# A four-layer graph network on one core: attention rows scattered whole in f32, and the counting pass with one accumulator

## The chip, the cores and the metric

The kernel runs on one NeuronCore of one Trainium2 chip. The metric is the device time of one execution in microseconds (us). Five engines work side by side from queues of their own: TensorE (PE; its weight loads are listed as PEld), VectorE (DVE), ScalarE (ACT), GpSimd (POOL) and SyncE (SP), which here only starts transfers. They wait for each other by semaphores.

## The reference, cut to what matters

The graph has 6250 nodes with 64 features and 206,250 edges (src, dst). Four layers follow each other, each on relu(layernorm(x)), each added to x. The first two are the ones that the change touches:

```python
# layer 0: attention, 4 heads of 16 channels
h = (x @ W).reshape(n, HEADS, CH)
e = leaky_relu(a_src[src] + a_dst[dst], NEG_SLOPE)
e = exp(e - segment_max(e, dst)[dst])
s = segment_sum(e, dst)
out = segment_sum(h[src] * (e / s[dst])[:, :, None], dst)
# layer 1: sum over the neighbours, divided by the root of the degree
agg = segment_sum(vertices[src], dst)
deg = segment_sum(ones, dst)
agg = agg * (clip(deg, 1.0, None) ** (-0.5))[:, None]
return agg @ weight.T + bias
```

Layer 2 sums rows weighted by edge_weight, and layer 3 runs two relational convolutions.

## The kernel before, in words

The nodes lie in 49 windows of 128. A first stage sorts the edges on the chip, so that the edges into one window of destinations stand in 50 columns of 128 edges (column c holds edges whose source is in window c, and column 49 the overflow). A window's columns are worked in 6 groups of 10, 8, 8, 8, 8 and 8 columns. Then come the passes over all 49 windows: attention, count, weight, and two relation passes. Each is a hardware loop over windows, whose body holds the six groups written out; each engine's queue is in order, and the semaphores named below are all that ties one engine to another.

**Gather and scatter are products with one-hot matrices.** A gather product takes the one-hot matrix of a column's sources (OT) and the rows of a window, and gives a row for each edge; a scatter product takes the one-hot matrix of the destinations (OD) and the edges' rows, and sums them into the 128 nodes of the window. Since products of bf16 are not exact enough for f32 rows, a row is split into three bf16 parts (high, middle, low) whose sum is the f32 number: Hp holds a window's rows as three parts.

**Attention pass** (`edge_pass`). For a column, PE's `gather` issues three products of 72 columns (L1157: 64 features and 8 scores, three parts) and three of 8 columns (L1161: the destination's part of the score, from `tab`, into the last 8 columns). DVE takes the scores (`scores`, L2040), ACT the exponent (`exponents`, L826), and DVE multiplies the rows by it (`weigh`, L2052) into Wf, 68 f32 columns for each edge. To scatter, Wf is split: ACT copies the high part (`highest`, L817), DVE subtracts it (`rest`, L2075), ACT copies the middle part (`middle`, L822), POOL subtracts again for the low part (`lowest`, L637). PE's `scatter` (L1175) then issues one bf16 product of 204 columns for each column of edges, and three more (L1182) for the few edges left over by the sort. The three parts of the sum stand side by side in PSUM; `evict` adds them on DVE (L2084) and adds the result to agg (L2090), twice for each window, as groups 0 to 2 use one PSUM bank and groups 3 to 5 another. DVE also makes both one-hot matrices (L2023 for OT, from codes that a DMA brings; L1657, a helper's line that every pass uses, for OD) and three small ones for the left-over edges (`few`, L2095).

On PE the body goes: gather of group g+2, scatter of group g. On DVE: `weigh` g, the OT matrix of g+3, `rest` g, `scores` g+1, the OD matrix of g+1, and an `evict` behind groups 2 and 5. A gather waits for `weigh` two groups before it (two sets of PSUM banks), a scatter for f_low of POOL.

**Count pass** (`count_pass`). PE builds a 128x128 matrix of edge counts for each column from two one-hot matrices (`build`, L1289), ACT copies it to bf16 (L884), and PE applies it to Hp (`apply`, L1304, 193 columns: three parts of 64, and a column of ones that gives the degree); L1311 is for the left-over edges. Groups 0 to 2 sum in PSUM bank 6 and groups 3 to 5 in bank 7. DVE makes both one-hot matrices of a group (L1657 twice), and evicts each bank with three instructions (L2272, L2276, L2277), each of which waits for the one before (`flink`); the evictions stand behind groups 2 and 5.

**Weight pass** (`weight_pass`, not changed). Groups 0, 2 and 4 of a window are scattered whole: an f32 one-hot matrix times f32 rows of 64 columns (L1229, and L1236 for the left-over edges), and groups 1, 3 and 5 in three bf16 parts (L1247, 192 columns). Its gather is L1215, three products of 64 columns for each column. An f32 product shows in the trace as two weight loads and two matmuls.

## Time and profile before

| what | value |
|---|---|
| median of 3 runs | 6114.63 us (6114.55 to 6117.37) |
| the profiled execution, its own time | 6114.21 us |
| its span in the trace | 6112.5 us |
| busy in the span: PE, DVE, ACT, POOL | 4598.9, 4985.0, 3358.9, 1454.7 us |
| attention pass, about | 1530 to 2732 us |
| count pass, about | 2795 to 3336 us |
| weight pass, about | 3399 to 4076 us |

A busy share is of one engine in one stretch. Matmuls overlap in their records, since the end of one is later than the start of the next; so the price of one in a row of them is the distance from start to start, not its mean duration. PEclk is the clock that TensorE was granted, as a share of its full speed.

### The profile page before, as it was taken

The numbers are of one execution on the slowest core, as the hardware profiler recorded it, in microseconds if no ns is written. First come the engines' busy times: TensorE is split into PE (matmuls) and PEld (weight loads), VectorE is DVE, ScalarE is ACT, GpSimd is POOL, SyncE is SP. The second block draws the span as 40 slices with busy tenths as digits, with TensorE's granted clock in tenths as the row PEclk, the third lists the DMA queues.
The fourth block names the chain that finished last, engine by engine and source line by source line (L and its number), as shares of the span: only waits on it lengthen the run. The fifth ranks groups of instructions, "written<-read, shape, count | busy, mean of one in ns | idle before, by whom it ended". The sixth has DMA issues, their size and how long they took to land.

```text
span 6112.5 us, 245738 instructions
## 1 busy us (share of the span) xinstructions
PE 4598.9 (75%) x91050; PEld 3703.5 (61%) x91050; DVE 4985.0 (82%) x10975; ACT 3358.9 (55%) x9701; POOL 1454.7 (24%) x2032
## 2 busy tenths in 40 slices
PE   2566666663777777765776799978999997999997
PEld 1343444342667666754666799976666665666665
DVE  8999999998999999998888899986666665666665
ACT  3566666562333333335666333346777776777776
POOL 2555555552333333320000222210000000000000
PEclk7677777776777778778999899989999998999999
DMA  1000000000666666640000344423232322333322
GB/s 43 1 1 1 1 1 1 1 1 16 216 200 203 202 202 201 203 150 11 0 0 0 108 118 118 120 73 93 84 84 84 84 84 78 84 84 85 84 84 75
DMA packets 305216, 501.29 MB, mean 82 GB/s; under 512 B 76918, under 2 KB 78454, under 8 KB 305126
## 3 DMA queue, kind: packets, MB, share of 16 engines
q1 hardware_dynamic: 303782, 499.39, 28.0%
q8 instruction: 59, 0.97, 0.1%
q0 software_dynamic: 576, 0.52, 0.0%
q10 hardware_dynamic: 768, 0.16, 0.0%
q14 instruction: 31, 0.25, 0.0%
HBM read 408.40 MB, written 91.57 MB: 82 GB/s over the span
## 4 chain that ended last, share of the span: by engine, by line
issue 54%; DVE 30%; PE 6%; POOL 6%; DVEq 2%; DMA 1%; ACT 1%; POOLq 0%; ACTq 0%; SPq 0%
DVE agg L1693 7%; DVE arena L1657 6%; POOL arena L637 5%; DVE Hp L1657 3%; DVE arena L1699 2%; DVE tmp L1657 2%; PE PS L1215 2%; PE PS L1229 1%; PE PS L1247 1%; DVE arena L2163 1%; DVE arena L2171 1%; PE PS L1236 1%; DVE arena L2272 1%; DVE arena L2282 0%; DVEq L1663 0%
## 5 line engine op out<-in xcount | busy, mean ns | idle before, releaser
L1657 DVE TENSOR_TENSOR arena<-iotab,arena 128x1024 bf16<-128x1024 bf16 (+6 forms) x1813 | 1688.5, 958 | 559.3 <-PE PS L1371 471.6
L932 ACT ACTIVATE arena<-PS 128x384 bf16<-128x384 f32 x2450 | 1077.2, 492 | 509.2 <-PE PS L1364 496.4
L1371 PE MATMUL PS<-arena 32*128 32x193 bf16 (+1 forms) x41552 | 1080.6, 243 | 1.2 <-ACT arena L932 1.2
L768 ACT ACTIVATE arena<-PS,m 128x196 bf16<-128x196 f32 x1813 | 743.5, 429 | 548.8 <-POOLq L537 328.5
L1371 PEld LDWEIGHTS PS<-arena 32*128 32x128 bf16 x41552 | 815.6, 93 | 180.2 <-issue 140.4
L1364 PE MATMUL PS<-Hp,arena 128*128 128x192 bf16 (+1 forms) x4900 | 662.5, 250 | 114.0 <-DMA arena<-hots 58.9
L1045 PE MATMUL PS<-arena,tmp 128*128 128x262 bf16 x1813 | 507.2, 328 | 294.3 <-DVE tmp L1657 293.1
L1037 PE MATMUL PS<-agg,onesb 128*128 128x196 bf16 x1715 | 514.4, 301 | 200.4 <-ACT arena L768 195.9
L1157 PE MATMUL PS<-Hp,arena 128*128 128x72 bf16 x7350 | 548.3, 214 | 63.3 <-DVE arena L2023 40.7
L1038 PE MATMUL PS<-Hp,own_b 128*128 128x196 bf16 x1813 | 545.9, 305 | 55.1 <-DVE Hp L1657 53.8
L714 POOL TENSOR_TENSOR arena<-arena 128x512 bf16<-128x512 f32 x98 | 168.8, 1722 | 1743.4 <-ACT arena L942 1743.4
L637 POOL TENSOR_TENSOR arena<-arena 128x544 bf16<-128x544 f32 (+1 forms) x294 | 391.5, 1332 | 797.1 <-ACT arena L822 796.9
L1175 PE MATMUL PS<-arena 128*128 128x204 bf16 x2450 | 351.1, 302 | 285.1 <-POOL arena L637 283.9
L1364 PEld LDWEIGHTS PS<-Hp,arena 128*128 128x128 bf16 x4900 | 326.4, 98 | 343.8 <-ACT arena L932 151.4
L1161 PE MATMUL PS<-tab,arena 128*128 (+1 forms) x7350 | 530.2, 172 | 0.0
L913 ACT ACTIVATE arena<-PS,ewB 128x64 f32<-128x64 f32 x1176 | 257.4, 330 | 428.1 <-PE PS L1215 428.1
L1157 PEld LDWEIGHTS PS<-Hp,arena 128*128 128x128 bf16 x7350 | 436.5, 105 | 90.5 <-DVE arena L2023 40.8
L1693 DVE TENSOR_TENSOR agg<-Hp,agg 128x196 bf16<-128x196 bf16 x1666 | 458.6, 275 | 17.1
L817 ACT ACTIVATE arena<-arena 128x544 bf16<-128x544 f32 (+1 forms) x294 | 198.7, 676 | 484.8 <-DVE arena L2052 484.8
L1161 PEld LDWEIGHTS PS<-tab,arena 128*128 128x128 bf16 x7350 | 459.3, 109 | 4.8
L1175 PEld LDWEIGHTS PS<-arena 128*128 128x128 bf16 x2450 | 249.7, 116 | 320.2 <-issue 218.1
L1045 PEld LDWEIGHTS PS<-arena,tmp 128*128 128x128 bf16 x1813 | 200.2, 113 | 376.9 <-DVE tmp L1657 358.5
(362 smaller groups left out, 9065.4 us busy)
## 6 DMA issues: line engine op xcount, KB each, us to landing
arena<-hots SPq DMA_DIRECT2D x735, 256.0 KB, 2.6
arena<-codes SPq DMA_DIRECT2D x245, 512.0 KB
hots<-arena SPq DMA_DIRECT2D x245, 256.0 KB, 4.2
arena<-hots SPq DMA_DIRECT2D x147, 320.0 KB, 2.9
arena<-codes SPq DMA_DIRECT2D x49, 640.0 KB
hots<-arena SPq DMA_DIRECT2D x49, 320.0 KB, 4.5
rows_h<-Hn SPq DMA_DIRECT2D x4, 1568.0 KB, 9.2
rows_l<-Y SPq DMA_DIRECT2D x1, 1764.0 KB, 10.4
```

The lines of the kernel that those rows point to most:

```text
L637: pool.tensor_tensor(W3[g % 2][:, 0:sz, 2 * v:3 * v], Rf[g % 2][:, 0:sz, 0:v], W3[g % 2][:, 0:sz, v:2 * v], ALU.subtract).then_inc(f_low, 1)
L768: act.activation(junk[:, j % 4, :], ps[j % 4][:, 0:KEYS], ACT.Relu, bias=m256[:, 0:1], accum_out=rank[:, j:j + 1]).then_inc(k_rank, 1)
L932: act.activation(RG[g % 2][:, 2 * i:2 * i + 2, 0:RW], ps[q % 2][:, 0:2 * RW].rearrange("p (k c) -> p k c", k=2), ACT.Copy).then_inc(r_ev, 1)
L1038: pe.matmul(to, own_b[:, :], OK[:, j, :], start=(j == 0), stop=True).then_inc(k_pref, 1)
L1045: pe.matmul(ps[4][:, 0:EW + 2], OS[:, j, :], E[:, j, 0:EW + 2], start=(j == 0), stop=(j == NJ - 1)).then_inc(k_perm, 1)
L1157: last = pe.matmul(to[:, 0:v], (OT if attends else w_OT)[g % 3][:, k * P:(k + 1) * P], rhs, start=(a == 0), stop=(a == PARTS - 1 and not a ...
L1161: last = pe.matmul(to[:, DIM:WIDE], OT[g % 3][:, (sz + k) * P:(sz + k + 1) * P], tab[:, bass.ds(dx * 24 + a * 8, 8)], start=False, stop=(a ...
L1175: last = pe.matmul(to, OD[g % 3][:, k, :], W3[g % 2][:, k, 0:used], start=(g % 3 == 0 and k == 0), stop=(g == 2 and k == GS[g] - 1))
L1364: last = pe.matmul(ps[q % 2][:, (k % 2) * RW:(k % 2 + 1) * RW], rOT[g % 3][:, k * P:(k + 1) * P], rhs, start=True, stop=True)
L1371: last = pe.matmul(ps[2 + q][:, b * SW:b * SW + SW - o], one_hot[32 * q:32 * q + 32, b * P:(b + 1) * P], rows_of[32 * q:32 * q + 32, 0:SW ...
L1657: return dve.tensor_tensor(to.rearrange("p k (n t) -> p k n t", t=4), iota_of[:, 0:n].rearrange("p (n t) -> p n t", t=4)[:, None, :, :] .t ...
L1693: dve.tensor_tensor(CU[:, j, :], OK[:, j, :], (OK if j == 1 else CU)[:, j - 1, :], ALU.add).then_inc(k_cum, 1)
```

## The change

- **Attention.** Rows are scattered whole: OD becomes an f32 matrix and Wf the second operand, and one f32 product of 68 columns stands for the bf16 one of 204. `highest`, `middle`, `rest` and `lowest` go. DVE still makes the one-hot matrix in bf16 (ODb, two buffers), and ACT turns it into f32 (`one_hots_whole`, L818 of the new file). The eviction is a single add from PSUM. The products with `tab` take 72 columns instead of 8, from ztab, a copy of a window's scores padded with zeros, which POOL makes once for each window (`table_of`); the gather of a window's first group waits for it (f_tab), and POOL waits for the last gather of the window before.
- **Count.** Hp holds 65 columns for each part (64 and a one, or a zero), so an apply product has 195 columns and one reduction gives sum and degree. All six groups sum in one PSUM bank, evicted once for each window behind group 1 of the next; the first apply of a window waits for it. The three small comparisons of `few` become one.
- The weight pass and what follows are as they were.

```diff
+        ODb = [cv.take(GS[0] * P, bf16).rearrange("p (k n) -> p k n", n=P) for _ in range(2)]
+        OD = [cv.take(GS[0] * P).rearrange("p (k n) -> p k n", n=P) for _ in range(3)]
...
+                def table_of(dx):
+
+                    if not is_zero(dx):
+                        pool.wait_ge(f_gath, dx * NG + 3)
+                        pool.sem_inc(s_held, 1)
+                    pool.tensor_copy(ztab[:, :, DIM:WIDE],
+                                     tab[:, bass.ds(dx * 24, 24)].rearrange("p (a c) -> p a c", a=PARTS)).then_inc(f_tab, 1)
...
                 with pool.Fori(1, WINDOWS) as d:
-                    for g in range(NG):
-                        lowest(0, d, g, WV)
+                    table_of(d)
...
             def exponents(dx, g):
                 act.wait_ge(f_mx, dx * NG + g + 1)
-                act.activation(Wf[g % 2][:, 0:GS[g], DIM:WV], mx[g % 2][:, 0:GS[g], :], ACT.Exp).then_inc(f_exp, 1)
+                act.wait_ge(f_scat, dx * NG + g + 1)
+                act.activation(Wf[g % 3][:, 0:GS[g], DIM:WV], mx[g % 2][:, 0:GS[g], :], ACT.Exp).then_inc(f_exp, 1)
...
+            def one_hots_whole(dx, g):
+
+                act.wait_ge(f_ohb, dx * NG + g + 1)
+                act.wait_ge(f_scat, dx * NG + g + 1)
+                act.activation(OD[g % 3][:, 0:GS[g], :], ODb[g % 2][:, 0:GS[g], :], ACT.Copy).then_inc(f_ohd, 1)
...
+                    if g == 0:
+                        pe.wait_ge(f_tab, dx + 1)
...
                         for a in range(PARTS):
-                            last = pe.matmul(to[:, DIM:WIDE], OT[g % 3][:, (sz + k) * P:(sz + k + 1) * P],
-                                             tab[:, bass.ds(dx * 24 + a * 8, 8)], start=False, stop=(a == PARTS - 1))
+                            last = pe.matmul(to[:, 0:WIDE], OT[g % 3][:, (sz + k) * P:(sz + k + 1) * P],
+                                             ztab[:, a, :], start=False, stop=(a == PARTS - 1))
...
-                pe.wait_ge(f_low, n + (order * NN + 3))
+                to = ps[4 + h][:, 0:rows_of[0].shape[2]]
+                pe.wait_ge(f_whole, n + (2 * order * NN + 3))
                 pe.wait_ge(f_ohd, n + (2 * order * NN + 1))
                 if g % 3 == 0:
...
-                    last = pe.matmul(to, OD[g % 3][:, k, :], W3[g % 2][:, k, 0:used], start=(g % 3 == 0 and k == 0),
+                    last = pe.matmul(to, hot[g % 3][:, k, :], rows_of[g % 3][:, k, :], start=(g % 3 == 0 and k == 0),
                                      stop=(g == 2 and k == GS[g] - 1))
...
             def apply(dx, g):
                 n = dx * NG + g
-                h = g // 3
-                to = ps[6 + h][:, 0:CW]
+                to = ps[6][:, 0:CW]
...
-                if g % 3 == 0:
-                    pe.wait_ge(f_accout, dx * 2 + (2 * WINDOWS + h + 1))
+                if g == 0:
+                    pe.wait_ge(f_accout, dx * 2 + (2 * WINDOWS + 2))
...
-                    last = pe.matmul(to, AB[g % 3][:, k * P:(k + 1) * P], rhs, start=(g % 3 == 0 and k == 0),
-                                     stop=(g == 2 and k == GS[g] - 1))
+                    last = pe.matmul(to, AB[g % 3][:, k * P:(k + 1) * P], rhs, start=(g == 0 and k == 0), stop=False)
...
+            def attention_pass(ofs):
                 def one_hots(dx, g):
                     if g == 0:
+                        if not is_zero(dx):
+                            dve.wait_ge(f_ohb, dx * NG)
                         flink(dve.tensor_copy(cdw, fours(cdA3[:, bass.ds(dx, 1), :].rearrange("p w c -> p (w c)"))))
-                    dve.wait_ge(f_scat, dx * NG + (2 * order * NN + g + 1))
-                    compare(OD[g % 3][:, 0:GS[g], :], iotab1, cdw[:, G0[g]:G0[g] + GS[g], :]).then_inc(f_ohd, 1)
+                    if g > 1:
+                        dve.wait_ge(f_ohd, dx * NG + g - 1)
+                    elif not is_zero(dx):
+                        dve.wait_ge(f_ohd, dx * NG + g - 1)
+                    compare(ODb[g % 2][:, 0:GS[g], :], iotab1, cdw[:, G0[g]:G0[g] + GS[g], :]).then_inc(f_ohb, 1)
...
-                def rest(dx, g):
...
-                    dve.wait_ge(f_high, n + 1)
...
-                    dve.wait_ge(f_low, n + 1)
-                    dve.tensor_tensor(Rf[g % 2][:, 0:sz, 0:v], Wf[g % 2][:, 0:sz, 0:v], W3[g % 2][:, 0:sz, 0:v],
-                                      ALU.subtract).then_inc(f_rest, 1)
...
-                        dve.wait_ge(f_sum, dx + (2 * order * WINDOWS + 1))
-                    got = ps[4 + h]
-                    flink(dve.tensor_reduce(part[:, 0:v], got[:, 0:3 * v].rearrange("p (a c) -> p c a", a=PARTS),
-                                            AX.X, ALU.add))
...
-                    flink(dve.tensor_tensor(to, to, part[:, 0:v], ALU.add))
+                        dve.wait_ge(f_sum, dx + 1)
+                    to = agg[:, bass.ds(dx, 1), 0:WV].rearrange("p w c -> p (w c)")
+                    flink(dve.tensor_tensor(to, to, ps[4 + h][:, 0:WV], ALU.add))
                     dve.sem_inc(f_accout, 1)
...
+            for a in range(PARTS):
+                dve.memset(Hp[:, :, a * CV + DIM:(a + 1) * CV], float(a == 0))
...
-                def evict(dx, h):
-                    if h == 0:
-                        dve.wait_ge(f_scat, dx * NG + (NN + 3 + 3))
-                    else:
-                        dve.wait_ge(f_sum, dx + (WINDOWS + 1))
-                    got = ps[6 + h]
-                    flink(dve.tensor_reduce(c_part[:, 0:DIM], got[:, 0:RW].rearrange("p (a c) -> p c a", a=PARTS),
-                                            AX.X, ALU.add))
-                    to = agg[:, bass.ds(dx, 1), 0:DIM].rearrange("p w c -> p (w c)")
-                    degree = agg[:, bass.ds(dx, 1), DIM:DIM + 1].rearrange("p w c -> p (w c)")
-                    flink(dve.tensor_tensor(degree, degree, got[:, RW:CW], ALU.add))
-                    flink(dve.tensor_tensor(to, to, c_part[:, 0:DIM], ALU.add))
-                    dve.sem_inc(f_accout, 1)
+                def evict(dx):
+                    dve.wait_ge(f_sum, dx + (WINDOWS + 1))
+                    flink(dve.tensor_reduce(c_part, ps[6][:, 0:CW].rearrange("p (a c) -> p c a", a=PARTS), AX.X, ALU.add))
+                    dve.sem_inc(f_accout, 2)
+                    to = agg[:, bass.ds(dx, 1), 0:CV].rearrange("p w c -> p (w c)")
+                    flink(dve.tensor_tensor(to, to, c_part, ALU.add))
...
+                    dve.tensor_tensor(c_OM, iota[:, 0:P][:, None, :].to_broadcast((P, MC, P)),
+                                      bc(msrel[:, bass.ds(dx, 1), :].rearrange("p w c -> p (w c)"), P),
+                                      ALU.is_equal).then_inc(f_ohm, 1)
...
-                        if g == 2 and not first:
-                            evict(dx - 1, 1)
+                        if g == 1 and not first:
+                            evict(dx - 1)
                         if g == 3:
                             few(dx)
-                        if g == 5:
-                            evict(dx, 0)
```

**Where instructions stand now.** PE in the attention pass, the end of one gather, a scatter, and the start of the next gather (the parts of the arena are named alike; Hp are the rows, PS is PSUM). Before:

```order
L1157 MATMUL PS<-Hp,arena 128x72 x3
L1161 MATMUL PS<-tab,arena 128x8 x3
L1175 MATMUL PS<-arena 128x204 [waits f_accout,f_ohd,f_low]
L1175 MATMUL PS<-arena 128x204 x9
L1157 MATMUL PS<-Hp,arena 128x72 [waits f_whole,f_oht]
L1157 MATMUL PS<-Hp,arena 128x72 x2
L1161 MATMUL PS<-tab,arena 128x8 x3
```

The same place now:

```order
L1152 MATMUL PS<-Hp,arena 128x72 x3
L1156 MATMUL PS<-arena 128x72 x3
L1170 MATMUL PS<-arena 128x68 [waits f_accout,f_ohd,f_whole]
L1170 MATMUL PS<-arena 128x68 x9
L1152 MATMUL PS<-Hp,arena 128x72 [waits f_whole,f_oht]
L1152 MATMUL PS<-Hp,arena 128x72 x2
L1156 MATMUL PS<-arena 128x72 x3
```

The order is the same; the scatter has rows of 68 columns and waits for f_whole (DVE) in place of f_low (POOL), and the products from tab are as wide as the others.

DVE in the attention pass, one group (L2052 is `weigh`, L2023 the OT matrix, L2075 `rest`, L2040 `scores`, L1657 the OD matrix). Before:

```order
L2052 TENSOR_TENSOR arena<-PS,arena 128x4x64 [waits f_exp]
L2052 TENSOR_TENSOR arena<-PS,arena 128x4x64
L2023 TENSOR_SCALAR arena<-arena,pidx 128x2048 [waits f_gath,f_kept1,f_bc1]
L2075 TENSOR_TENSOR arena<-arena 128x544 [waits f_low,f_high]
L2037 REGISTER_ALU
L2040 TENSOR_REDUCE arena<-PS 128x16 [waits f_gath]
L2040 TENSOR_REDUCE arena<-PS 128x16
L2033 REGISTER_ALU
L1657 TENSOR_TENSOR arena<-iotab,arena 128x1024 [waits f_scat]
```

Now:

```order
L2045 TENSOR_TENSOR arena<-PS,arena 128x4x64 [waits f_exp]
L2045 TENSOR_TENSOR arena<-PS,arena 128x4x64
L2016 TENSOR_SCALAR arena<-arena,pidx 128x2048 [waits f_gath,f_kept1,f_bc1]
L2032 REGISTER_ALU
L2035 TENSOR_REDUCE arena<-PS 128x16 [waits f_gath]
L2035 TENSOR_REDUCE arena<-PS 128x16
L1650 TENSOR_TENSOR arena<-iotab,arena 128x1024 [waits f_ohd]
```

L2075 with its two waits is gone, and the OD matrix waits for ACT (f_ohd) in place of PE's scatter.

DVE in the count pass, the matrices of group 2 of a window and the eviction behind them (L2272 to L2277; a second eviction stands behind group 5; L2014 and L2260 are steps of the links between dependent instructions). Before:

```order
L1657 TENSOR_TENSOR arena<-iotab,arena 128x1024 [waits f_gath]
L1657 TENSOR_TENSOR arena<-iotab,arena 128x1024
L2270 REGISTER_ALU
L2272 TENSOR_REDUCE arena<-PS 128x64 [waits f_sum]
L2014 REGISTER_ALU
L2276 ISA [waits f_step]
L2276 TENSOR_TENSOR agg<-agg,PS 128x1
L2014 REGISTER_ALU
L2277 ISA [waits f_step]
L2277 TENSOR_TENSOR agg<-agg,arena 128x64
L2014 REGISTER_ALU
L2260 REGISTER_ALU [waits f_step]
```

Now, the matrices of group 1, the eviction behind them, and the first of group 2:

```order
L1650 TENSOR_TENSOR arena<-iotab,arena 128x1024 [waits f_gath]
L1650 TENSOR_TENSOR arena<-iotab,arena 128x1024
L2231 REGISTER_ALU
L2232 TENSOR_REDUCE arena<-PS 128x65 [waits f_sum]
L2007 REGISTER_ALU
L2235 ISA [waits f_step]
L2235 TENSOR_TENSOR agg<-agg,arena 128x65
L2007 REGISTER_ALU
L2225 REGISTER_ALU [waits f_step]
L1650 TENSOR_TENSOR arena<-iotab,arena 128x1024 [waits f_gath]
```

One eviction of two instructions stands there for two of three, one group earlier, and it waits for f_sum, PE's last product of the window before.

## Rows read from the trace of the kernel before

**Rows 1.** Stretches: PE, PEld, DVE, ACT, POOL busy us; PEclk; DMA share; GB/s.
```profile
1600.00:2700.00 1100.00, 820.73 (x15908) 759.13 (x15909) 1025.61 (x2256) 398.10 (x811) 360.92 (x271) 0.79 0.66 202
2800.00:3300.00 500.00, 373.88 (x4684) 325.26 (x4682) 428.54 (x949) 327.70 (x545) 2.77 (x4) 0.99 0.00 0
3450.00:4000.00 550.00, 525.58 (x9270) 520.85 (x9267) 501.15 (x720) 210.13 (x960) 124.87 (x120) 1.00 0.42 119
```
**Rows 2.** Lines of few in the three passes: ns least/median/greatest, first and last start.
```profile
L2095 DVE TENSOR_SCALAR arena<-iotab,mrel x147: 240/249/1220, 1550.5 to 2722.3; 128x128 bf16<-128x128 bf16 x147
L2282 DVE TENSOR_SCALAR arena<-iotab,msrel x147: 240/249/251, 2799.4 to 3330.6; 128x128 bf16<-128x128 bf16 x147
L2191 DVE TENSOR_TENSOR arena<-iota,mrel x49: 553/1159/1248, 3406.0 to 4066.5; 128x384 f32<-128x384 f32 x49
```
**Rows 3.** Timeline of DVE in attention: start us, duration us, instruction.
```profile
2017.11 0.72 DVE L2075 TENSOR_TENSOR arena<-arena 128x544 f32<-128x544 f32 x1
2017.76 0.28 DVE L2040 TENSOR_REDUCE arena<-PS 128x16 f32<-128x32 f32 x2
```
**Rows 4.** Timeline of PE in attention: a gather column, a scatter (idle before in brackets).
```profile
2001.32 0.26 PE L1157 MATMUL PS<-Hp,arena 128*128 128x72 bf16 x3
2001.41 0.22 PE L1161 MATMUL PS<-tab,arena 128*128 x3
2001.49 0.26 PE L1157 MATMUL PS<-Hp,arena 128*128 128x72 bf16 x3
...
2004.91 1.06 PE L1175 MATMUL PS<-arena 128*128 128x204 bf16 x10 [2.58 <-POOL arena L637]
2005.81 0.26 PE L1157 MATMUL PS<-Hp,arena 128*128 128x72 bf16 x3
```
**Rows 5.** Timeline of PE in the weight pass.
```profile
3602.72 0.86 PE L1247 MATMUL PS<-arena 128*128 128x192 bf16 x8 [0.62 <-DVEq L2186]
...
3604.29 1.98 PE L1229 MATMUL PS<-arena 128*128 128x64 f32 x16
3606.10 0.83 PE L1236 MATMUL PS<-arena 128*128 128x64 f32 x6
3606.77 0.86 PE L1215 MATMUL PS<-Hp,arena 128*128 128x64 bf16 x24
3607.47 0.85 PE L1247 MATMUL PS<-arena 128*128 128x192 bf16 x8
```
**Rows 6.** Weight loads, f32 and bf16: ns least/median/greatest, first and last start.
```profile
L1229 PEld LDWEIGHTS PS<-arena x2548: 188/192/192, 3403.9 to 4073.4; 128*128 128x128 f32 x196
L1215 PEld LDWEIGHTS PS<-Hp,arena x7350: 95/98/153, 3399.1 to 4070.2; 128*128 128x128 bf16 x199
```
**Rows 7.** Timeline of ACT in count: the copy of eight columns.
```profile
3001.61 1.02 ACT L884 ACTIVATE arena<-PS 128x1024 bf16<-128x1024 f32 x1 [0.67 <-PE PS L1289]
```
**Rows 8.** A small instruction of POOL in the sort: busy us, mean ns.
```profile
L547 POOL TENSOR_TENSOR arena<-arena 128x4 f32<-128x4 f32 x49 | 21.8, 445 | 3.8
```
**Rows 9.** Timeline of DVE in count, most of a window.
```profile
3003.66 3.97 DVE L1657 TENSOR_TENSOR arena<-iotab,arena 128x1280 bf16<-128x1280 bf16 x6 [0.61 <-DVE agg L2277]
3007.54 0.35 DVE L2272 TENSOR_REDUCE arena<-PS 128x64 f32<-128x192 f32 x1
3008.08 0.16 DVE L2276 TENSOR_TENSOR agg<-agg,PS 128x1 f32 x1 [0.18 <-DVE arena L2272]
3008.36 0.23 DVE L2277 TENSOR_TENSOR agg<-agg,arena 128x64 f32 x1
3008.90 1.29 DVE L1657 TENSOR_TENSOR arena<-iotab,arena 128x1024 bf16<-128x1024 bf16 x2 [0.31 <-DVE agg L2277]
3010.11 0.57 DVE L2282 TENSOR_SCALAR arena<-iotab,msrel 128x128 bf16<-128x128 bf16 x3
```
**Rows 10.** Timeline of PE in count, over the window's end.
```profile
3005.28 0.73 PE L1289 MATMUL PS<-arena 128*128 128x128 bf16 x10 [1.74 <-DVE arena L1657]
3006.51 0.42 PE L1311 MATMUL PS<-arena 128*128 128x193 bf16 x3
```

182 lines of the change are left out of this document (64 added, 118 removed).

## The prediction, made before the changed kernel ran

> **What bounds the kernel now.** I read the busy time by stretch first [rows 1]. In attention DVE works 1025.6 of 1100 us (93%), PE 820.7 (75%), ACT 398.1 and POOL 360.9. In count DVE works 86% and PE 75%. In the weight pass PE works 525.6 of 550 us (96%) and DVE 91%. So DVE sets attention and count, PE nearly sets the weight pass. The lengths come from the lines of `few`, which run once (three instructions) or once (one instruction) in a window [rows 2]: (2722.3 - 1550.5)/48 = 24.41 us for a window of attention, less a few hundredths, as the last start is the third of its three: 24.39; in the same way 11.06 for count and 13.76 for the weight pass. Then the timeline of PE in attention [rows 4]: before a scatter it stands still for up to 2.58 us until POOL has the low part. A column of the gather takes 0.17 us from start to start (2001.32 to 2001.49), and a scatter product 0.90/10 = 0.09. So PE's work for a window at full clock is 50 x 0.17 + 53 x 0.09 = 13.3 us of the 24.39 (53: 50 columns and 3 for left-over edges), the rest is waiting and time at half clock.
>
> **Attention, PE.** The work grows. The three products of 8 columns become three of 72. 24 products of 64 columns take 3607.47 - 3606.77 = 0.70 us, 0.029 each [rows 5]; eight columns more at 2.4 GHz are 0.003, and the three of 72 columns in attention take 0.09 [rows 4], 0.030 each. I take 0.032: 6 x 0.032 = 0.192 us for a column in place of 0.17, and 50 x 0.192 = 9.6 us. The f32 product is the large term. In the weight pass 16 records take 3606.10 - 3604.29 = 1.81 us and 6 records 0.67 [rows 5]: 0.112 each, and a column has two, 0.224. These have 64 columns of rows, the new ones 68. A record holds a weight load and the stream of its columns. If all of it were stream, it would grow by 68/64, to 0.238 for a column; if the load set it, it would stay at 0.224. I take the middle, 0.230, because the load of f32 is long (192 ns against 98 for bf16 [rows 6]) and cannot be all hidden; so 53 x 0.230 = 12.2 us, between 11.9 and 12.6. Seams: a weight window of 13.76 us with 0.62 idle [rows 2, 5] leaves 13.14 for 150 x 0.029 + 29 x 0.224 + 24 bf16 scatters at 0.09 = 13.0, so about 0.15. Sum for PE: 9.6 + 12.2 + 0.15 = **22.0 us** a window.
>
> A rule of the Trainium skill speaks to that middle value: "TensorE: Matmul & The Clock Gate", section "LDWEIGHTS (loading the stationary operand)", gives a load as its columns divided by 1.2, thus an estimate of 107 ns for 128, nearly the whole record of 112. By that the wider rows would cost nothing. The rows show only the 112 together. The sum by it would use 0.224.
>
> **Attention, DVE.** It works 1025.6/1100 x 24.39 = 22.7 us a window now. The six L2075 go, 2017.76 - 2017.11 = 0.65 each [rows 3]: 3.9 us. The reduction of both evictions goes too, and whatever DVE loses beside POOL's six instructions, which go. So DVE keeps 18.8 us at most, without counting these, and is below PE's 22.0. What it saves beyond that is worth nothing, since PE is now last.
>
> **Attention, ACT and POOL.** ACT loses two copies for each group and gains one of 1024 elements. Nearest is the copy of 1024 elements from PSUM in count, 1.02 us [rows 7]: 6 x 1.02 and a little more for the group of ten are 6.4 us, beside the exponents; it works under 9 of 22 us. The copy stands behind the exponent of its group and ahead of the next one, whose scores come a whole group later, so nobody waits for it. PE needs `weigh` of group g before the gather of g+2. Its scores can start when the gather of g has ended; till then PE has two scatters (1.84 us each) and one gather (1.54), 5.2 us. DVE's share of a group is 22.7/6 = 3.8 us now, evictions and all, and less afterwards. It is hidden.
>
> The new wait for POOL's table: POOL may start when the last gather of a window has ended; the first gather of the next window stands behind the scatter of group 3, 8 x 0.230 = 1.84 us. A small instruction of POOL takes 0.45 us [rows 8]. I cost it at nothing; with the cover gone it is 0.45 x 49 = 22 us.
>
> The gain of attention: 24.39 - 22.0 = 2.39 us, x 49 windows = **117 us**.
>
> **Count.** DVE sets it. Six comparisons take 3007.54 - 3003.66 = 3.88 us, and a pair of 1024 elements 3010.11 - 3008.90 = 1.21 [rows 9], so the pair of group 0 takes 1.46 and all twelve 1.46 + 5 x 1.21 = 7.51. Now two evictions of three linked instructions are added (1.36 us the one from 3007.54 to 3008.90, longer at the loop's end, where 0.61 us are idle). Afterwards there is one of two: 0.54 for the reduction and its link, 0.54 for the add and its link, 1.08. The three comparisons of `few` take 0.57; the one that replaces them has 384 elements in f32. Its like in the weight pass takes 0.55 at least and 1.16 in the median [rows 2]; there POOL works and here it doesn't (2.77 us in 500 [rows 1]), so I take 0.5, and the range keeps 1.1. Sum 7.51 + 1.08 + 0.5 = 9.1 us.
>
> To that comes a new wait. The eviction stands behind group 1 and waits for f_sum. DVE has done group 0 at 3003.66 + 1.46 = 3005.12; PE then builds (3005.28), applies the last group of the window before, and ends the left-over products at 3006.51 + 0.42 = 3006.93 [rows 10], 1.8 us after. DVE has only the pair of group 1 (1.21) before it gets there, so it stands still for 0.6 us, and behind it in its queue stand the comparisons of groups 2 to 5. PE itself waits little: it has the build of group 1 ahead of the apply that needs the bank. A window takes 9.7 us. The gain is 1.36 x 49 = **67 us**. Between 9.1 (no wait) and 10.3 (the slow comparison) it would be 96 or 37.
>
> **The rest.** Sort, weight and relation passes are not touched. Hp's new layout costs some instructions once; a few tenths. The sum: 6112.5 - 117 - 67 = 5928.5 us of span. The profiled execution lies 1.7 us above its span and 0.4 below the median, so 5930.
>
> **The rivals.**
> 1. PE does not run unbroken. The table is not hidden (0.45), the f32 product costs 0.238 and a wide product 0.195/6: 9.75 + 12.6 + 0.15 + 0.45 = 22.95 us, 47 us more than forecast: 5977. For it: weight windows idle 0.62 us although both engines are near full. Against: there DVE is at 91%, here under 86%.
> 2. The f32 product costs 0.224 (the load sets it) and the seams vanish: 9.6 + 11.9 = 21.5 us, 5906; the load's rule named above, alone, gives 12.2 - 11.9 = 0.3 less a window and 5915.
> 3. The one bank in count makes a chain: PE waits for DVE's eviction and DVE for PE's sum, and the wait is 2 us and not 0.6. Then count stays at 11.06: 5997. Against: PE has only some 7 us of work in a window there.
> 4. Slower: the clock. In attention PE was granted 0.79 [rows 1]; its work is now 49 x 22.0 = 1078 us at full clock, and at a granted 0.79 it takes 1365 instead of today's 49 x 24.39 = 1195: 170 - 67 = 103 us slower, 6217. It decides from a clock under 1078/(1195 + 67) = 0.85. For it: in count PE is just as busy (75%) and was granted 0.99, so the busy share does not tell the clock. Against: attention's scatters come after up to 2.58 us of standing still, which go, and the weight pass, half of it the same f32 products, was granted 1.00.
> The Trainium skill ("TensorE: Matmul & The Clock Gate", section "HAM oscillation — how this bites in real kernels") says that it is idle gaps between bursts that bring the half clock back; the rows of attention and of the weight pass agree.
> 5. Nothing comes of it, within 0.2%, for a reason that I don't see.
>
> **How the numbers follow.** Forecast 0.66, rival 1 0.12, rival 2 0.08, rival 3 0.06, rival 4 0.05, rival 5 0.03. The likeliest time is 5930. From 5890 to 5985 the range takes in rivals 1 and 2 and the bounds of the single terms (96 or 37 for count, 24 less or 47 more for attention), 0.86 in all; rival 3 lies just outside. Faster by more than 0.2%, which is about what a measurement of this kernel can tell: 0.92; within: 0.03; slower: 0.05.
>
> **What would show it.** PE above 95% busy and a clock near 1.00 in attention; the lines of `few` 22.0 us apart there and 9.7 in count; f32 records of 0.115 us from start to start; DVE waiting for PE's gather at `scores`; in count a wait of 0.6 us before L2232; no wait of PE for POOL. If DVE is still at 90% in attention, the sum for DVE was wrong; if the clock is under 0.9, rival 4 holds in part; if the wait before L2232 is above 1 us, rival 3 does.

## The result, and the profile of the changed kernel

The changed kernel takes 5921.0 us (median of 4 runs, 5919.1 to 5922.8) against 6115.3 us before. The ratio on record is 0.9677, 95% interval 0.9665 to 0.9689 (the two medians alone give 0.9682). The forecast was 5930. The profiled execution took 5919.13 us, its span is 5917.4 us.

Stretches of the changed kernel, core 0, in attention, count and weight pass (columns as in [rows 1]):

```profile
1600.00:2600.00 1000.00, 1000.00 (x18633) 1000.00 (x18633) 683.14 (x1927) 365.40 (x551) 33.32 (x45) 1.00 0.71 223
2680.00:3080.00 400.00, 350.08 (x4312) 292.62 (x4310) 360.87 (x628) 298.67 (x504) 0.00 (x0) 1.00 0.00 0
3250.00:3800.00 550.00, 525.80 (x9259) 521.18 (x9260) 501.52 (x719) 210.08 (x960) 124.97 (x120) 1.00 0.43 119
```

In attention the two engines have changed places: PE is busy for all of the 1000 us, at a granted clock of 1.00 in place of 0.79, and DVE for 68% in place of 93%. The line that takes the scores shows who waits for whom (busy us, mean ns, idle of DVE before it and what ended it): in the kernel before (1600 to 2700 us) DVE never stood still for PE's gather, in the changed one (1600 to 2600 us) it does for 274.1 us.

```profile
L2040 DVE TENSOR_REDUCE arena<-PS 128x16 f32<-128x32 f32 (+1 forms) x540 | 75.9, 181 | 0.0
```

```profile
L2035 DVE TENSOR_REDUCE arena<-PS 128x16 f32<-128x32 f32 x550 | 79.9, 188 | 274.1 <-PE PS L1156 274.1
```

The weight pass is as it was. The length of a window comes from lines that run once or three times in each: `few` in attention (L2062), and the eviction of count (L2232) with what it waited for.

```profile
L2062 DVE TENSOR_SCALAR arena<-iotab,mrel x147: 279/282/289, 1548.3 to 2593.1; 128x128 f32<-128x128 bf16 x147
...
L2232 DVE TENSOR_REDUCE arena<-PS x49: 361/364/364, 2676.6 to 3135.9; 128x65 f32<-128x195 f32 x49
its engine sat idle before it (us, times) until:
  PE PS L1304: 29.9, 49
```

In attention that is (2593.1 - 1548.3)/48 = 21.77 us, less the few hundredths of [rows 2]: 21.75. In count it is (3135.9 - 2676.6)/48 = 9.57, where it was 11.06. The eviction waits 29.9/49 = 0.61 us for PE's last sum.

PE's timeline in attention, the place of [rows 4]: a scatter, then the gather of eight columns with no idle time in brackets anywhere, then the next scatter.

```profile
2001.20 1.98 PE L1170 MATMUL PS<-arena 128*128 128x68 f32 x16
2003.02 0.26 PE L1152 MATMUL PS<-Hp,arena 128*128 128x72 bf16 x3
2003.12 0.26 PE L1156 MATMUL PS<-arena 128*128 128x72 bf16 x3
2003.21 0.26 PE L1152 MATMUL PS<-Hp,arena 128*128 128x72 bf16 x3
...
2004.48 0.26 PE L1156 MATMUL PS<-arena 128*128 128x72 bf16 x3
2004.58 0.64 PE L1170 MATMUL PS<-arena 128*128 128x68 f32 x4
```

**Where the time went.** Attention gave back (24.39 - 21.75) x 49 = 129 us, count (11.06 - 9.57) x 49 = 73, together 202. The span fell by 6112.5 - 5917.4 = 195.1. The difference of 7 is in the second relation pass, which the change does not touch. The line that fills it is L1371 before and L1364 after (first and last start in that pass); before:

```profile
L1371 PE MATMUL PS<-arena x20776: 238/242/363, 5137.7 to 6086.0; 32*128 32x192 bf16 x200
```

After:

```profile
L1364 PE MATMUL PS<-arena x20776: 237/242/364, 4935.7 to 5890.9; 32*128 32x192 bf16 x200
```

It lasts 948.3 us before and 955.2 after, 6.9 more. The end of the section on the experiments comes back to it.

### The profile page after: what moved, and what is told of

It reads as the page before. It is cut to its first block, busy times and chain, and to the rows that moved or that the text cites. A ratio compares the mean times of both kernels' runs of the same rounds, so it can differ in the third digit from the quotient of the medians.

```text
span 5917.4 us, 248557 instructions
## 1 busy us (share of the span) xinstructions
PE 4783.7 (81%) x93647; PEld 3944.7 (67%) x93647; DVE 4563.0 (77%) x10291; ACT 3312.4 (56%) x9407; POOL 1096.9 (19%) x1785
## 4 chain that ended last, share of the span: by engine, by line
issue 41%; DVE 29%; PE 25%; DVEq 2%; DMA 1%; ACT 1%; POOL 1%; POOLq 0%; ACTq 0%; SPq 0%
PE PS L1170 9%; DVE agg L1686 7%; DVE arena L1650 6%; PE PS L1152 4%; PE PS L1156 4%; DVE Hp L1650 3%; DVE arena L1692 2%; DVE tmp L1650 2%; PE PS L1210 2%; PE PS L1224 1%; PE PS L1242 1%; DVE arena L2126 1%; DVE arena L2134 1%; PE PS L1284 1%; PE PS L1298 1%
## 5 line engine op out<-in xcount | busy, mean ns | idle before, releaser
L1364 PE MATMUL PS<-arena 32*128 32x193 bf16 (+1 forms) x41552 | 1080.6, 243 | 1.2 <-ACT arena L925 1.2
L1364 PEld LDWEIGHTS PS<-arena 32*128 32x128 bf16 x41552 | 815.6, 93 | 180.4 <-issue 140.3
L1170 PE MATMUL PS<-arena 128*128 128x68 f32 x4900 | 603.4, 277 | 0.0
L1170 PEld LDWEIGHTS PS<-arena 128*128 128x128 f32 x4900 | 570.9, 192 | 0.0
L1152 PE MATMUL PS<-Hp,arena 128*128 128x72 bf16 x7350 | 499.2, 198 | 41.7 <-DVE arena L2016 40.6
L1156 PE MATMUL PS<-arena 128*128 128x72 bf16 x7350 | 499.9, 198 | 0.0
L1030 PEld LDWEIGHTS PS<-agg,onesb 128*128 128x128 bf16 x1715 | 189.1, 110 | 371.3 <-ACT arena L764 304.0
L1156 PEld LDWEIGHTS PS<-arena 128*128 128x128 bf16 x7350 | 405.3, 100 | 0.0
L1692 DVE TENSOR_TENSOR arena<-arena 128x520 bf16<-128x520 bf16 (+1 forms) x931 | 396.9, 426 | 1.3 <-POOLq L568 1.0
```

Of the source, the lines that this page charges most:

```text
L1030: pe.matmul(to, onesb[:, :], (OK if j == 1 else CU)[:, j - 1, :], start=True, stop=False)
L1152: last = pe.matmul(to[:, 0:v], (OT if attends else w_OT)[g % 3][:, k * P:(k + 1) * P], rhs, start=(a == 0), stop=(a == PARTS - 1 and not a ...
L1156: last = pe.matmul(to[:, 0:WIDE], OT[g % 3][:, (sz + k) * P:(sz + k + 1) * P], ztab[:, a, :], start=False, stop=(a == PARTS - 1))
L1170: last = pe.matmul(to, hot[g % 3][:, k, :], rows_of[g % 3][:, k, :], start=(g % 3 == 0 and k == 0), stop=(g == 2 and k == GS[g] - 1))
L1364: last = pe.matmul(ps[2 + q][:, b * SW:b * SW + SW - o], one_hot[32 * q:32 * q + 32, b * P:(b + 1) * P], rows_of[32 * q:32 * q + 32, 0:SW ...
```

## Experiments

All edits are to the changed kernel unless it says otherwise, and "window" is one of the 49. A "record" is one MATMUL entry of the trace; an f32 product has two. Runs 1, 5, 9, 11 and 12 have four executions or more, the others one. Executions of one kernel on one chip lay up to 12 us apart (the kernel before: 6114.3 to 6126.2), so runs with one execution are read by the lengths of their windows in the trace, and by the total only where it differs by far more. Two questions stood ahead. Was the sum for attention right for its reasons: DVE off the path, and the full clock because PE no longer stands still? And what is the eviction in count worth, by its number and by its place?

### 1. The table's products narrow again

```diff
-   last = pe.matmul(to[:, 0:WIDE], OT[...], ztab[:, a, :], start=False, ...)
+   last = pe.matmul(to[:, DIM:WIDE], OT[...], ztab[:, a, DIM:WIDE], start=False, ...)
```

> The changed kernel, but the products with the table take its 8 columns again and not 72 with zeros; the table is still made by POOL. Sum theory (attention is PE's work at full clock): a gather column goes from 0.1955 us back to 0.173, so a window loses 50 x 0.0225 = 1.1 us, from 21.75 to about 20.65, 54 us in all: about 5867 us, at a granted clock of 1.00. Rival (the narrow products were what brought half clock, and the wide ones are there for that): the clock in attention falls to about 0.8, a window takes 20.6/0.8 = 25.8 us, and the kernel is some 195 us slower than the changed one, about 6116.

Measured: 6623.8 us, ratio 1.0833 to the kernel before (interval 1.0814 to 1.0851), 703 us slower than the changed kernel. The stretch of attention, then the PEclk line of the page (the granted clock in 40 slices of the span, in tenths) of this kernel and of the changed one:

```profile
1600.00:2600.00 1000.00, 1000.00 (x11232) 1000.00 (x11230) 414.68 (x1161) 219.64 (x332) 19.91 (x27) 0.50 0.45 136
```

```profile
PEclk7777777775555555555589989998999999999999
```

```profile
PEclk7777777777899999989998999989999998999999
```

PE is busy without a break and was granted the lower of its two levels, 1.2 GHz, all through attention. A window takes 36.13 us. So the sum theory fell, and the rival held in kind: it had the sign, but half clock is 0.50 here and not 0.8. The reason that I had given for the full clock fell with it. There is no standing still in this run, and yet no full clock.

### 2 and 3. The low part's load back on POOL, and the wait for it

```diff
+   for i in range(3):      # on POOL, for each group, after the rows are weighed
+       pool.wait_ge(f_dum, n * 3 + (i + 3))
+       pool.tensor_tensor(scr[:, 0:400], scr[:, 0:400], scr[:, 0:400], ALU.mult).then_inc(f_dum, 1)
```

and in the second run also

```diff
    pe.wait_ge(f_whole, n + (2 * order * NN + 3))
+   pe.wait_ge(f_dum, n * 3 + 6)
```

> The changed kernel, with three f32 products of 400 elements on POOL for each group of attention, on a scratch tile that nobody reads and nobody waits for, about the load that the low part was. Theory: DVE slows beside POOL (the OT matrix from 0.75 to about 1.1 us or more, 3 to 5 us more DVE work for each window, 14.9 to about 19), and the window stays at 21.75 us since PE is last: 5921 within 10. Rival (DVE is still close to the path): the window grows to 22.5 us or more, 5958 or more.

> The same load on POOL, and PE's scatter of each group waits for it, as it waited for the low part before the change. POOL needs about 2.8 us after the rows are weighed, PE has 1.56 us of gather meanwhile, so PE stands about 1.2 us before each scatter, 7.5 us for each window. Theory A (standing still brings half clock, whatever the products are): the granted clock in attention falls to 0.8 or so, and a window takes 21.6/0.8 + 7.5 = 34.5 us: about 6540. Theory B (the f32 and wide products keep the clock): the clock stays at 1.00 and a window takes 29.2 us: about 6285.

Measured: 5920.6 us with the load alone, 5961.9 with the wait. First the stretch of attention with the load alone, then the OD matrix on DVE there (busy us, mean ns, idle before) and in the changed kernel, last the stretch with the wait:

```profile
1600.00:2600.00 1000.00, 1000.00 (x18633) 1000.00 (x18632) 879.63 (x1929) 365.45 (x552) 923.94 (x874) 1.00 0.71 223
```

```profile
L1674 DVE TENSOR_TENSOR arena<-iotab,arena 128x1024 bf16<-128x1024 bf16 (+1 forms) x276 | 303.5, 1100 | 5.7
```

```profile
L1650 DVE TENSOR_TENSOR arena<-iotab,arena 128x1024 bf16<-128x1024 bf16 (+1 forms) x276 | 195.1, 707 | 5.7
```

```profile
1600.00:2600.00 1000.00, 972.35 (x18007) 966.63 (x18004) 825.40 (x1864) 351.78 (x533) 900.80 (x843) 1.00 0.70 218
```

The load alone makes DVE work 88% in place of 68%, with the same instructions: the OD matrix takes 1100 ns in place of 707 beside POOL. It costs no time, since PE is last. That is the first theory: 4.3 us more DVE work for each window, and the time unmoved. The OT matrix, which I had named, is the smaller part of it (850 ns in place of 769); the three comparisons of `few` went from 282 to 672. The run with the wait told little: PE's queue was far enough behind DVE that it stood only 27.6 us in 1000, the clock stayed at 1.00, and a window took about 22.55 us, 0.8 more. My 1.2 us before each scatter left out that the rows are weighed a scatter earlier than the gather begins.

### 4. A wait that is long enough

The same with five POOL products for each group instead of three.

> The changed kernel with five POOL products of 400 elements for each group of attention instead of three, and the scatter waits for them. In the run with three, 1.09 us each, PE stood only 0.7 us once or twice in a window. Five are 5.5 us for a group, 33 us for a window, more than PE's 21.75: PE must stand still for a third of the time, 1.5 to 2 us before each scatter. Theory A (the wide products keep the clock, standing still does not take it): granted clock 0.95 or more and a window of 33 us, set by POOL. Theory B (standing still takes it): granted clock 0.8 or less, and the window may be longer than 33 us.

Measured: 6478.4 us; a window takes 33.1 us, POOL's own time. The stretch of attention, and one scatter in PE's timeline:

```profile
1600.00:3100.00 1500.00, 1276.07 (x18416) 1255.05 (x18414) 857.59 (x1905) 360.13 (x544) 1379.01 (x1406) 0.81 0.48 149
```

```profile
2002.37 3.68 PE L1195 MATMUL PS<-arena 128*128 128x68 f32 x16 [2.67 <-POOL arena L658]
```

The row shows 2.67 us of standing still before a scatter; the longest in the stretch is 3.3. The granted clock is 0.81 with the wide products too. It is theory B by the clock; it cost nothing here, as POOL sets the window. So standing still does take the clock. It is a second cause beside the one of run 1.

### 5. The kernel before, with the gather of the changed one

```diff
-   last = pe.matmul(to[:, DIM:WIDE], OT[...], tab[:, bass.ds(dx * 24 + a * 8, 8)], ...)
+   last = pe.matmul(to[:, 0:WIDE], OT[...], Hp[:, bass.ds(dx, 1), a * v:(a + 1) * v]..., ...)
```

> The kernel before, with one thing changed: the three narrow products of a gather column take 72 columns of Hp (the window's own rows) in place of 8 of the table, so the scores and the output are others, and their time is that of the changed kernel's gather. Theory A (the width of the gather's products gives the clock, in any scatter): the granted clock in attention rises from 0.79 to 0.95 or more. The window is then 24.39 us only if DVE and the chain over POOL set it; if half clock was part of it, it shrinks, by 1 us or more, 50 us in all or more: 6065 or less. Theory B (the stalls before the scatter, up to 2.58 us, give the clock, and they stay): 0.79 stays and the 1.1 us more of PE's work per window are paid in part: 6115 to 6180.

Measured: 6121.0 us beside 6118.3 of the kernel before on the same chip, ratio 0.9999 (0.9990 to 1.0009): the same. Attention:

```profile
1600.00:2700.00 1100.00, 775.75 (x15921) 711.78 (x15919) 1024.48 (x2254) 398.15 (x811) 360.80 (x270) 0.95 0.66 201
```

The clock rises from 0.79 [rows 1] to 0.95, PE's busy time falls, and DVE's is the same to a thousandth (1025.6 before). The time does not move. That isolates what the prediction began with: in the kernel before, PE's clock cost nothing, and DVE, busy for 93%, set attention. In the changed kernel, where PE sets it, the clock is everything.

The clock is theory A's, and it says more than that. PE's waits for POOL in that stretch (us in total, times, longest), first in the kernel before, then here:

```profile
PE PS L1175 <- POOL arena L637: 258.2, 184, 2.6
```

```profile
PE PS L1175 <- POOL arena L637: 297.3, 215, 2.4
```

The standing still did not go. PE was idle for 1100 - 775.75 = 324 us here and for 279 in the kernel before, and yet the clock rose from 0.79 to 0.95. So most of what was missing there came from the narrow products, and at most the rest, 0.05, from the waits. Nor does the share of idle time tell the clock: it was 29% here at 0.95, and 15% in run 4 at 0.81. The longest wait was 2.4 us here and 3.3 in run 4, but the products differ too, and no run separates the two.

### 6 and 7. What an f32 record's columns cost, and what they do to the clock

```diff
-   last = pe.matmul(to, hot[g % 3][:, k, :], rows_of[g % 3][:, k, :], ...)
+   j = min(k, GS[g] - 3)
+   last = pe.matmul(ps[4 + h][:, 0:204], hot[g % 3][:, k, :], rows_of[g % 3][:, j:j + 3, :]..., ...)
```

The first run has this alone, the second has it with the narrow table products of run 1. Only the products of the 50 columns are widened, the 3 for left-over edges stay at 68 columns.

> The changed kernel, with f32 scatter products of 204 columns (the rows of three columns of edges side by side; only the first 68 columns of the sum are used, and for the last two columns of a group they are those of another column, so the output differs). It prices the stream of an f32 record. If a record of 0.112 us is set by its weight load and the stream takes one cycle a column (85 ns for 204), it stays at 0.112 and the window at 21.75 us. If the stream takes two cycles a column (170 ns), a record goes to 0.17 or more, 106 of them add 6.2 us or more, and a window is 28 us: 6220 in all.

> The products with the table take 8 columns, as in the run that had half clock throughout (a window of 36.13 us), and the f32 scatter products 204 columns as in the run beside this one. Theory A (it is the 8-column products that take the clock): the clock stays at 0.50 and the window at 36 us or more: 6620 or more. Theory B (it is how much PE streams over all its products, so wide ones elsewhere make up for narrow ones): the clock is 0.95 or more, and the window is that of the run beside this one less 1.1 us.

Measured: 6231.3 and 6180.3 us. Both have a granted clock of 1.00:

```profile
1600.00:2800.00 1200.00, 1200.00 (x17373) 1183.97 (x17371) 641.22 (x1797) 339.08 (x512) 31.84 (x43) 1.00 0.56 175
```

```profile
1600.00:2750.00 1150.00, 1150.00 (x17291) 1134.05 (x17289) 637.94 (x1786) 337.46 (x510) 31.79 (x43) 1.00 0.59 182
```

A scatter of the first run, 16 records, and the gather that follows it:

```profile
2003.70 3.00 PE L1171 MATMUL PS<-arena 128*128 128x204 f32 x16
2006.54 0.26 PE L1152 MATMUL PS<-Hp,arena 128*128 128x72 bf16 x3
```

The windows are 28.09 and 27.05 us. The first is 6.34 over 21.75. My expectation divided by 106 records, but only 100 were widened: 0.063 for each, so 0.175 us for one of 204 columns, against 0.112 for one of 68. The rows agree: 2006.54 - 2003.70 = 2.84 us for 16, where the changed kernel has 2003.02 - 2001.20 = 1.82. That is two cycles of 2.4 GHz for each column (0.170) and 0.005, so the second price of the expectation holds. At 68 columns two cycles a column would be 0.057, far under the 0.112 that the record takes. The difference of the two runs, 1.04 us a window, is what the 64 columns of zeros in the table's products cost. And the narrow products had the full clock here: theory B. They do not take the clock as such.

### 8. Does the clock follow the products, or stay?

The table's products take 72 columns in the first 16 windows and 8 in the other 33.

```diff
-   with pe.Fori(0, LASTW) as d:
-       body(d, False)
+   with pe.Fori(0, 16) as d:
+       body(d, False)
+   lead[0] = False         # from here the gather writes and reads 8 columns
+   with pe.Fori(16, LASTW) as d:
+       body(d, False)
```

> The changed kernel, with the table's products of 72 columns in the first 16 windows of attention and of 8 columns in the other 33 (the scatter stays at 68 columns). The kernel with 8 columns throughout entered attention at a granted clock of 0.50 and never left it, at 36.13 us a window. Theory A (a full clock once granted stays while PE stands nowhere still): 1.00 to the end, 33 windows at 20.7 us, 5921 - 34 = 5887. Theory B (the clock follows the products that PE is at, whatever it was before): it falls to 0.50 soon after window 16, 33 windows at 36.13 us, 5921 + 33 x 14.4 = 6396. Theory C: it swings between the two, with a time between.

Measured: 5883.1 us. The stretch after window 16, and the lines of `few` in it:

```profile
1900.00:2560.00 660.00, 660.00 (x12937) 660.00 (x12937) 473.88 (x1337) 253.10 (x383) 23.62 (x32) 1.00 0.75 235
```

```profile
L2069 DVE TENSOR_SCALAR arena<-iotab,mrel x93: 277/277/278, 1939.0 to 2560.4; 128x128 f32<-128x128 bf16 x93
```

31 windows with (2560.4 - 1939.0)/30 = 20.71 us each, at 1.00. On PE they are the same products, in the same order and as unbroken, as those of run 1, which were granted 0.50. Only what came before differs: run 1 came to attention at 0.50 out of the sort, with PE idle from 1500 to 1530 us. So theory A holds. At this width of products the clock stayed at the level that it had, for 33 windows at 1.00 here and for 49 at 0.50 in run 1, and the wide products were needed to get it up, not to keep it.

### 9 and 10. The eviction in count: its place and its number

```diff
-   if g == 1 and not first:
+   if g == 2 and not first:
        evict(dx - 1)
```

In the second run the sum lies in two banks again, evicted behind groups 2 and 5 of a window, by the two instructions of the changed kernel each.

> The changed kernel, but the one eviction of the counting pass stands behind the matrices of group 2 in DVE's queue and not behind those of group 1. Theory A (only DVE counts): its wait of 0.61 us for PE's last sum goes, a window takes 9.58 - 0.61 = 8.97 us, 30 us less: about 5891. Theory B (PE is near full too, its 100 products and 3 are some 8.8 us of 9.58): the first apply of a window has to wait for the bank until DVE has made group 2's matrices, about 1.4 us of standing still, and a window takes about 10.2 us: 30 us more, about 5951.

> The changed kernel, with the counting pass's two sums and two evictions of two instructions each again, behind groups 2 and 5, each waiting only for sums that PE ended a while ago; the 195 columns and the single comparison for the left-over edges stay. DVE's work by the rows of the changed kernel is 8.97 us, and a second eviction adds 0.36 + 0.23 and two links, about 1.0 us: 10.0 us a window, 20 us over the changed kernel, 5941. If the new wait of 0.6 us and not the number of evictions had set the window, it would be 9.0 us and 5893.

Measured: 5894.2 us (ratio 0.9638, 0.9622 to 0.9654) and 5964.6 us. DVE with the eviction behind group 2, then with two evictions:

```profile
2799.68 4.57 DVE L1650 TENSOR_TENSOR arena<-iotab,arena 128x1024 bf16<-128x1024 bf16 x7
2804.16 0.36 DVE L2232 TENSOR_REDUCE arena<-PS 128x65 f32<-128x195 f32 x1
2804.78 0.23 DVE L2235 TENSOR_TENSOR agg<-agg,arena 128x65 f32 x1 [0.26 <-DVE arena L2232]
2805.22 1.29 DVE L1650 TENSOR_TENSOR arena<-iotab,arena 128x1024 bf16<-128x1024 bf16 x2 [0.21 <-DVE agg L2235]
```

```profile
2802.10 0.35 DVE L2237 TENSOR_REDUCE arena<-PS 128x65 f32<-128x195 f32 x1
2802.69 0.23 DVE L2240 TENSOR_TENSOR agg<-agg,arena 128x65 f32 x1 [0.24 <-DVE arena L2237]
2803.66 3.97 DVE L1652 TENSOR_TENSOR arena<-iotab,arena 128x1280 bf16<-128x1280 bf16 x6 [0.74 <-DVE agg L2240]
2807.55 0.35 DVE L2237 TENSOR_REDUCE arena<-PS 128x65 f32<-128x195 f32 x1
...
2808.61 1.29 DVE L1652 TENSOR_TENSOR arena<-iotab,arena 128x1024 bf16<-128x1024 bf16 x2 [0.21 <-DVE agg L2240]
```

Behind group 2 the eviction waits for PE once in the whole pass (2.9 us) and otherwise not: a window takes 9.02 us, 0.55 less. Theory A holds, although PE's idle time is small; theory B had it that PE would pass the delay on, and it did not. With two evictions a window takes 10.62 us, 1.6 over 9.02, and not the 1.0 that I expected. The rows show why: an eviction behind group 2 takes 2808.61 - 2807.55 = 1.06 us of DVE's queue, one at the window's end 2803.66 - 2802.10 = 1.56, as 0.74 us pass between its last instruction and the first of the next window. So count's gain of 1.49 us a window has three parts: 11.06 - 10.62 = 0.44 from the shorter evictions and the single comparison, 1.6 from the eviction that is gone, and 0.55 given back to the new wait.

### 11 and 12. Two versions that beat both kernels

The first has f32 scatter products of 128 columns (the row and what follows it in memory; the sum uses 68) with narrow table products throughout; the second two windows of wide table products and then narrow ones. Both have the eviction behind group 2. The second is the edits of runs 8 and 9 with `Fori(0, 2)`; the scatter of the first:

```diff
-   last = pe.matmul(to, hot[g % 3][:, k, :], rows_of[g % 3][:, k, :], ...)
+   last = pe.matmul(ps[4 + h][:, 0:128], hot[g % 3][:, k, :], Wx[g % 3][:, k * WV:k * WV + 128], ...)
```

> Built from the runs so far: the products with the table take 8 columns; the f32 scatter products take 128 columns (the row of a column of edges and 60 elements of what follows it; only the first 68 columns of the sum are used, the output is the reference's); the eviction of the counting pass stands behind group 2. A record of 204 columns took 0.1725 us, about 2 cycles a column and 2.5 ns, so 128 columns would be 0.109, under the 0.112 that a record of 68 takes: the wider scatter costs nothing. If the clock holds as it did with 204 columns: attention 21.75 - 1.04 = 20.7 us a window, count 9.02: 5921 - 51 - 27 = 5843. If it does not hold and falls to 0.50 as with 68 columns: 36.1 us a window, about 6597.

> The version that the runs point to: the table's products take 72 columns in the first two windows of attention and 8 in the other 47, the f32 scatter stays at 68 columns, and the eviction of the counting pass stands behind group 2. In the run with 16 such windows the clock stayed at 1.00 for the other 33, at 20.70 us a window; in the changed kernel it was 1.00 from the second half of the first window on. If two windows are lead enough: 47 x (21.75 - 20.70) = 49 us less in attention and 27 less in count, 5921 - 76 = 5845, 13 us under the version with scatter products of 128 columns (5858.6). If the clock has to be held longer before the products narrow, it falls to 0.50 in attention and the time is about 6570.

Measured: 5858.6 us (ratio 0.9572, 0.9556 to 0.9588) and **5840.8 us** (5839.1 to 5842.2; ratio 0.9544, 0.9528 to 0.9560). Attention of the first and the second:

```profile
1600.00:2500.00 900.00, 900.00 (x17460) 897.50 (x17459) 641.33 (x1807) 341.56 (x517) 31.86 (x43) 1.00 0.75 235
```

```profile
1530.00:1580.00 50.00, 45.67 (x859) 45.42 (x860) 33.50 (x91) 16.66 (x27) 8.79 (x12) 0.92 0.86 273
1580.00:2500.00 920.00, 920.00 (x18051) 920.00 (x18047) 662.47 (x1866) 352.75 (x533) 32.48 (x44) 1.00 0.75 237
```

The clock holds in both. The windows of the first take 20.93 us and not 20.7: 100 records of 128 columns cost 0.23 us more than 100 of 68, so they are nearly free but not quite (0.114 us each). I had expected 0.109, from the 0.1725 of the wrong division; with 0.175 it would have been 0.112. Two wide windows are enough to lead in the second, which is 80 us under the changed kernel: 47 x 1.04 = 49 from attention and 27 from count. The 4 that are left lie in the second relation pass, which lasts 949.5 us here and 955.2 in the changed kernel. The same holds for run 8, which came 4 us under its expectation with a pass of 950.2.

**What stays open.** The second relation pass has two rhythms with the same instructions. A window of it takes 19.47 us in the kernel before and in runs 3, 4, 5, 8, 10 and 12, and 19.57 to 19.60 in the changed kernel and in runs 1, 2, 6, 7, 9 and 11. The extra 0.14 us stands before one product of PE in each window (L1408 of the changed kernel). No edit of mine goes with it, and what it depends on I didn't find. It is worth 4 to 7 us in the comparisons above between a run of one group and one of the other. The weight pass, too, can be some 7 us longer in one execution: 13.90 us a window instead of 13.76 in the profiled one of run 9, which at 5899.3 was the slowest of its four.

## Why the prediction came out right, step by step

- **DVE sets attention before.** Right. Run 5 shows that PE's clock does not: 0.95 instead of 0.79, and the same time. In the changed kernel DVE's `scores` wait 274.1 us for PE, where they had not waited at all.
- **DVE falls below PE.** Right, and by more than I counted: 683.14/1000 x 21.75 = 14.9 us a window where I had 18.8 at most. The means of single instructions in the two traces name the 3.9 between: the two reductions that went (360 ns each, 0.7), the OT matrix (949 ns before, 769 after; six, 1.1), the comparisons of `few` (572, 282; three, 0.9), and the add of the eviction (793, 219; two, 1.1). For the last three the obvious cause is POOL, which had worked beside them and hardly does now; I had named that and not counted it. Run 2 shows that such a load does slow the OT matrix (850) and `few` (672). Its add took 212, and the add's operand changed with the kernel too, so there POOL is not shown to be the cause. The 4.3 us of run 2 are like in size only: there it is mostly the OD matrix, which took 704 ns in the kernel before.
- **PE's sum, 22.0 us.** Measured 21.75. The gather has 2004.58 - 2003.02 = 1.56 us for eight columns, 0.195 each and 9.75 in all (I had 9.6). That leaves 12.0 for 53 f32 products with their seams, 0.226 each (I had 0.230 and 0.15 of seams). The four added columns of an f32 product cost nothing (1.82 us for 16 records, 1.81 in the weight pass [rows 5]), so the middle value that I took was 0.3 us too dear. Run 6 shows where the width begins to count: two cycles a column is under the record's 0.112 up to some 130 columns. The Trainium skill's rule for the load ("TensorE: Matmul & The Clock Gate", "LDWEIGHTS (loading the stationary operand)"), by which a load of 128 columns is an estimated 107 ns, agrees with the unchanged f32 record. That the load is what sets the record is argued and not shown; bf16 products, which load 128 columns as well, start every 1.56/48 = 0.033 us.
- **The clock at 1.00.** The value was right, but the reason given for it was the lesser part, and that it came out was luck. I argued that standing still had brought the half clock, and that it goes. Run 5 keeps it and has 0.95 in place of 0.79, and run 1 has none of it and 0.50. Run 4 does confirm that waits can take the clock (0.81). My other argument, that the weight pass has the same f32 products at 1.00, carries no weight either: run 1 has them at 0.50. What I had listed as a cost only, the 64 columns of zeros in each table product, is what brings the clock up from the 0.50 that the sort leaves. Without them, and with nothing else changed, rival 4 would have come true, and at 36.13 us a window far beyond its 6217. I had 0.05 on it; not knowing of the width, that was too little. The Trainium skill's section "HAM oscillation — how this bites in real kernels" ("TensorE: Matmul & The Clock Gate"), which names idle gaps, agrees with run 4 (0.81), and run 1 is not covered by it.
- **ACT and POOL are hidden.** Right: ACT works 365.4/1000 x 21.75 = 7.9 us a window, and PE waited for the table once in the pass, 0.6 us.
- **Count, 9.7 us, with a wait of 0.6.** Measured 9.57 and 0.61. The comparison for the left-over edges takes 0.55 (I had 0.5), and the rest 8.4 where I had summed 8.6. The wait was right in its cause too: run 9 moves the eviction by one group and it goes.
- **The sum.** 129 us in attention where I had 117, 73 in count where I had 67, and 7 lost in a pass that I took as fixed: 5921 against 5930. The two gains were each some 10% small, and the relation pass, in which I saw no term, hid a part of that. That the total came within 9 us is in part such cancelling.
- **The rivals.** In attention the measured 21.75 lies halfway between my 22.0 and the 21.5 of rival 2; nearest is rival 2 with the f32 product alone at 0.224, 21.7. Rival 1 did not come: PE ran unbroken. Rival 3's chain did not form: one wait of 0.61 us, which run 9 takes away by a single position in the queue.

## What to carry to other kernels

Before an engine is relieved, ask which engine becomes last, and whether its clock will be there: a clock that costs nothing while another engine sets the time (run 5) can cost 74% when it sets it (run 1: 36.13 us a window against 20.71). When PE is last, look at the granted clock at the entry of a pass as well as in its middle. If it comes in at half clock and does not rise, some wide products at the start may be all it needs, and paying for width in every window may not be. And in an in-order queue the place of an instruction that waits is worth a test of its own: one group later was worth 27 us here.

## What the runs showed of the hardware that I had not expected

- The same unbroken row of products ran at a granted clock of 0.50 for all 49 windows or at 1.00 for 33 (20.71 us a window against 36.13), by what PE had done before. With wide products it rose within the first window: 0.65 in the stretch from 1530 to 1540 us of the changed kernel, and 1.00 from 1540 to 1550.
- An f32 record of 68 columns takes as long as one of 64 (0.112 us), one of 128 takes 0.002 more, and one of 204 takes 0.175.
- PE was granted 0.95 while idle for 29% of attention (run 5), and 0.81 while idle for 15% (run 4).
- POOL working beside DVE makes DVE's one-hot matrix take 1100 ns instead of 707, and the whole of DVE's attention work 29% longer, on tiles that the two do not share.
